# Linear and softmax attention in one kernel: denominators packed by transfers, the keys' mean taken earlier, one state product per tile

## The reference, cut to what matters

```
xn = layernorm(x)                                   # [4, 2048, 512]
# 1: linear attention, 16 heads of 32
q, k = elu(xn @ wq) + 1, elu(xn @ wk) + 1;  v = xn @ wv
for every token: S += k (x) v;  z += k
    num = q . S;   den = q . z + 1e-6;   out1 = num / den
y1 = out1 @ wo
# 2: softmax attention over the whole sequence, 16 heads of 32
q, k, v = xn @ Wq.T + bq, xn @ Wk.T + bk, xn @ Wv.T + bv
q = (q / |q| + query_embedding) * softplus(temperature)
h = softmax(q . k / sqrt(32)) @ v
gates = softmax(h @ Wr.T + br), top 3, times a shared gate of softmax(h @ Ws.T + bs)
y2 = (h * sum(gates)) @ Wp.T + bp
result = x + y1 + y2
```

## Time and profile before

| | us |
|---|---|
| median of 3 | 4643.3 |
| profiled execution | 4645.28 |
| its span | 4643.5 |
| PE busy | 4076.4 (88%) |
| DVE busy | 3418.9 (74%) |
| ACT busy | 2650.1 (57%) |
| mean granted PE clock | 0.955 of full |

### The profile page before, as it was taken

The page is one execution under the profiler, slowest core; times in us unless marked ns, Lnnn a source line. Parts: engine busy times, 40 slices in busy tenths (PEclk is TensorE's granted clock), DMA queues, the critical chain, the costliest instruction groups (busy, mean ns, idle before and its releaser), DMA issues.

```text
span 4643.5 us, 94232 instructions
## 1 busy us (share of the span) xinstructions
PE 4076.4 (88%) x39532; PEld 1690.4 (36%) x39532; DVE 3418.9 (74%) x3549; ACT 2650.1 (57%) x3447; POOL 337.0 (7%) x210
## 2 busy tenths in 40 slices
PE   3489989898989999898999989899998989899768
PEld 1243333333333334333333433333343334333213
DVE  4537888887877878777787877788677767777773
ACT  3126666666656566565666656566665656566550
POOL 0100000000000000000000000000000000000001
PEclk7589999999999999999999999999999999999998
DMA  3421211112222212213221222322122121212115
GB/s 126 134 76 44 58 51 53 57 50 62 61 60 64 82 55 79 63 56 88 64 82 56 79 63 56 88 65 79 47 71 62 51 75 57 76 42 61 33 31 185
DMA packets 368043, 318.15 MB, mean 69 GB/s; under 512 B 157632, under 2 KB 316352, under 8 KB 366912
## 3 DMA queue, kind: packets, MB, share of 16 engines
q1 hardware_dynamic: 367552, 311.32, 22.9%
HBM read 236.25 MB, written 74.97 MB: 67 GB/s over the span
## 4 chain that ended last, share of the span: by engine, by line
PE 54%; DVE 14%; ACT 12%; issue 10%; DMA 9%; SPq 1%; POOL 0%; ACTq 0%; DVEq 0%
PE ps L912 10%; PE ps L926 10%; PE ps L795 10%; ACT prob L669 9%; DVE acc L1393 8%; PE ps L891 6%; DMA rq<-rq_scratch 6%; PE ps L803 5%; PE ps L843 2%; DMA rq_scratch<-rq_c 2%; PE ps L868 2%; PE ps L865 2%; PE ps L823 2%; PE ps L837 1%; PE ps L851 1%
## 5 line engine op out<-in xcount | busy, mean ns | idle before, releaser
L669 ACT ACTIVATE prob<-ps 128x1024 f32<-128x1024 f32 x2048 | 1984.6, 1023 | 939.3 <-PE ps L912 899.1
L1393 DVE TENSOR_TENSOR acc<-acc,prob 128x2048 f32<-128x2048 f32 x896 | 2047.4, 2285 | 76.4 <-ACT prob L669 63.0
L926 PE MATMUL ps<-prob,v 128*32 128x512 f32 x8192 | 1107.2, 613 | 1.1 <-ACT prob L669 1.1
L912 PE MATMUL ps<-q_hi,k_hi 32*128 32x512 f16 x4096 | 426.0, 388 | 306.5 <-ACT prob L669 230.2
L795 PE MATMUL ps<-x_hi,w_hi 128*128 128x512 f16 x1024 | 412.4, 403 | 9.5 <-issue 8.1
L912 PE MATMUL ps<-q_lo,k_hi 32*128 32x512 f16 x4096 | 415.9, 378 | 2.4 <-issue 2.4
L912 PE MATMUL ps<-q_hi,k_lo 32*128 32x512 f16 x4096 | 415.9, 379 | 2.0 <-issue 2.0
L795 PE MATMUL ps<-x_lo,w_hi 128*128 128x512 f16 x1024 | 408.7, 399 | 0.0
L795 PE MATMUL ps<-x_hi,w_lo 128*128 128x512 f16 x1024 | 407.7, 398 | 0.0
L912 PEld LDWEIGHTS ps<-q_hi,k_hi 32*128 32x128 f16 x4096 | 109.4, 91 | 676.3 <-ACT prob L669 461.8
L891 PE MATMUL ps<-wop_hi,fin 128*128 128x512 f16 x1024 | 325.7, 384 | 16.4 <-DVE st L1367 13.0
(11 more groups left out here) (248 smaller groups left out, 4466.5 us busy)
## 6 DMA issues: line engine op xcount, KB each, us to landing
x_hi<-xhi_scratch SPq DMA_DIRECT2D x64, 512.0 KB, 4.1
x_lo<-xlo_scratch SPq DMA_DIRECT2D x64, 512.0 KB, 5.2
x_in<-in_x SPq DMA_DIRECT2D x64, 256.0 KB, 5.4
rq<-rq_scratch SPq DMA_DIRECT2D x64, 256.0 KB
rdl<-rdl_scratch SPq DMA_DIRECT2D x64, 256.0 KB
rden<-rden_scratch SPq DMA_DIRECT2D x64, 256.0 KB
fin<-hhi_scratch SPq DMA_DIRECT2D x128, 128.0 KB, 3.5
fin<-hlo_scratch SPq DMA_DIRECT2D x128, 128.0 KB, 4.6
```

The source lines that it names most:

```text
L669: s_.activation(prob[i % 3][:, 2 * p:2 * p + 2, :], ps[:, 2 * p:2 * p + 2, :], ACT.Exp, bias=-SHIFT, scale=1.0 / CQK).then_inc(exped, 1)
L912: last = t_.matmul(bank[h], kk[rows32(h), cols128(kt)], qq[rows32(h), :], start=(kk is kh and qq is qh), stop=(kk is kl and not wide))
L926: last = t_.matmul(bank[OUT][rows32(h), :], v[m // NB % 2][:, kt, rows32(h)], prob[i % 3][:, h, :], start=(kt == 0), stop=(kt == TT - 1))
L1393: v_.tensor_tensor(acc[:], acc[:], prob[i % 3][:], ALU.add).then_inc(summed, 1)
```

## The change

The names on the left are the kernel's functions.

- `total` and `linear_den` no longer pack. `total` makes one 512-column product for each head against a column block of ones (`ones_v`), `linear_den` a single 512-column product against `blockden`; every channel row of a head then holds that head's denominator.
- ACT copies both from PSUM (`keep_den`, new, slot 1; `keep_dl` now 512 wide), and SP packs them by two transfers (`pack`, new: 4 rows of 512 to DRAM, back as 16 rows of 128). DVE takes the reciprocals of 16 x 128 values, in slots 2 and 5. Then the same spread as before.
- `numerators` uses one full 128 x 128 state product per tile. For that ACT writes the key-value products into `kvm`, whose off-diagonal blocks are cleared once (`keep_kv`, new, slot 13), and `states` adds from `kvm`. ACT copies the numerators out of X1 (`keep_num`, new, slot 3), and DVE divides that copy.
- `mean_k` and `shift_k` of the next round are done in slots 9 and 10 of the last step of the round before; those of the first round ahead of the steps.
- Slots: `divide_o` from 4 to 6, `split_o` from 4 and 5 to 6 and 7, `divide_h` from 5 to 8, `split_h` from 6 and 7 to 9 and 12, `scale_q` from 9 to 11, `split_q` from 9 and 10 to 12 and 13; in slot 14 the mask before the states; the sum over a tile of x (`sum_x`) from 6 to 7. SP's spread of the query norms is ahead of the stores of h and behind the load of the V weights.

```diff
-        den_l, den_h = sb("den_l", [P, BT, HG, BT, ROWS]), sb("den_h", [P, BT, BT, ROWS])
+        blockden, ones_v = sb("blockden", [P, P]), sb("ones_v", [P, HD])
...
+            def pack(dst, scratch_d, src, out_sem, in_sem, i):
+
+                sp.dma_start(scratch_d, src[::HD, :]).then_inc(out_sem, 16)
+                sp.wait_ge(out_sem, (i + 1) * 16)
+                sp.dma_start(dst[:], scratch_d.rearrange("h (t n) -> (h t) n", t=BT)).then_inc(in_sem, 16)
...
                 if p is not None:
-                    sp.wait_ge(rdl_done, p + 1)
-                    spread(rdl, rdl_d, rdl_c[::ROWS, :], rdl_out, rdl_in, p, o1_ready)
+                    sp.wait_ge(dl_kept, p + 1)
+                    pack(rdl_c, rdl_d, rdl, dl_out, dl_in, p)
...
             def keep_dl(p):
                 act.wait_ge(dl_mm, p + 1)
-                act.wait_ge(rdl_done, p)
-                s_.activation(dl[:], X1[:, 0:P], ACT.Identity, bias=eps1[:, 0:1]).then_inc(dl_kept, 1)
+                act.wait_ge(o1_ready, p)
+                s_.activation(rdl[:], X1, ACT.Identity, bias=eps1[:, 0:1]).then_inc(dl_kept, 1)
+
+            def keep_kv(n):
+
+                act.wait_ge(kv_done, n + 1)
+                if n:
+                    act.wait_ge(state_ready, states_after(n - 1))
+                act.wait_ge(kvm_cleared, 1)
+                for h in range(HG):
+                    ins = s_.activation(kvm[rows32(h), :, h, :], X1[rows32(h), :].rearrange("p (t n) -> p t n", t=BT)[:, :, rows32(h)],
+                                        ACT.Copy)
+                ins.then_inc(kv_kept, 1)
+
+            def keep_num(p):
+                act.wait_ge(num_done, p + 1)
+                act.wait_ge(olo_done, p)
+                s_.activation(o1[:], X1, ACT.Copy).then_inc(num_kept, 1)
...
+            def keep_den(m):
+                act.wait_ge(den_done, m + 1)
+                act.wait_ge(hm_done, m)
+                s_.activation(rden[:], X2, ACT.Copy).then_inc(den_kept, 1)
...
             def total(m):
                 pe.wait_ge(summed, (m + 1) * N_ADDS)
-                for j in range(BT):
-                    for h in range(HG):
-                        last = t_.matmul(X2[rows32(h), 0:P], den_h[:, j].rearrange("p t i -> p (t i)"), acc[:, h, cols128(j)],
-                                         start=(j == 0), stop=(j == BT - 1))
+                for h in range(HG):
+                    last = t_.matmul(X2[rows32(h), :], ones_v[:], acc[:, h, :], start=True, stop=True)
                 last.then_inc(den_done, 1)
 
             def linear_den(n):
                 pe.wait_ge(pz_ready, n + 1)
-                for j in range(BT):
-                    last = t_.matmul(X1[:, 0:P], den_l[:, j].rearrange("p h t i -> p (h t i)"), zc[:, cols128(j)], start=(j == 0),
-                                     stop=(j == BT - 1))
-                last.then_inc(dl_mm, 1)
+                t_.matmul(X1, blockden[:], zc[:], start=True, stop=True).then_inc(dl_mm, 1)
...
                     pe.wait_ge(state_ready, i + 1)
+                    t_.matmul(X1[:, cols128(j)], st[:, i % NST, :], phqT[:, cols128(j)], start=True, stop=True)
                     for h in range(HG):
-                        t_.matmul(X1[rows32(h), cols128(j)], st[rows32(h), i % NST, rows32(h)], phqT[rows32(h), cols128(j)],
-                                  start=True, stop=False)
-                    for h in range(HG):
-                        last = t_.matmul(X1[rows32(h), cols128(j)], vl[:, j, rows32(h)], am[:, h, j, :], start=False, stop=True)
+                        last = t_.matmul(X1[rows32(h), cols128(j)], vl[:, j, rows32(h)], am[:, h, j, :], start=False, stop=True,
+                                         skip_group_check=True)
...
-                        if n is not None and n % NB == 0:
-                            mean_k(n // NB)
                     if kt == 2 and n is not None:
                         if mp is not None:
-                            pe.wait_ge(rden_done, mp + 1)
+                            pe.wait_ge(den_kept, mp + 1)
...
                             if p is not None:
-                                pe.wait_ge(o1_ready, p + 1)
+                                pe.wait_ge(num_kept, p + 1)
...
                         project(X2, LQ_, n, (0, 1))
+                        if n % NB == NB - 1 and n < NBLK - 1:
+                            pe.wait_ge(kl_part, n + 1)
+                            mean_k(n // NB + 1)
...
             def invert_dl(p):
-                dve.wait_ge(dl_kept, p + 1)
-                dve.wait_ge(rdl_out, p * 16)
-                v_.reciprocal(rdl_c[:], dl[:]).then_inc(rdl_done, 1)
+                dve.wait_ge(dl_in, (p + 1) * 16)
+                v_.reciprocal(rdl_c[:], rdl_c[:]).then_inc(rdl_done, 1)
...
             def invert_den(m):
-                dve.wait_ge(den_done, m + 1)
-                dve.wait_ge(rden_out, m * 16)
-                v_.reciprocal(rden_c[:], X2[:, 0:P]).then_inc(rden_done, 1)
+                dve.wait_ge(den_in, (m + 1) * 16)
+                v_.reciprocal(rden_c[:], rden_c[:]).then_inc(rden_done, 1)
```

192 lines of the change are left out of this document (105 added, 87 removed).

## The result

The changed kernel takes 4511.4 us, the median of 4 executions (4503.9 to 4512.1), beside 4643.4 us (4640.8 to 4647.2) for the kernel before on the same chip: ratio 0.9711, with a 95% interval of 0.9694 to 0.9728. The forecast was 4520 us. Its profiled execution took 4503.88 us (span 4502.1 us, mean granted clock 0.966), 141.4 us less than that of before. Two executions far above the others of their kernels (6867 us of the kernel before, 4927 us of the one with late norms, at mean granted clocks of 0.65 and 0.82) are left out of the medians.

A forecast was written before the change was run, and what follows sets the result against it. PE, busy 88% of the span, was taken as the bound, with waits in slots 2, 9 and 10 and DVE pacing slots 11 to 13. Terms summed to -123.6 us from 4645.3, forecast 4520 us, range 4472 to 4588.

The forecast's parts named there:

- Keys' mean and X2: Slot 2 of first steps becomes ordinary without mean and reciprocal wait: -64.6 us, 32.9 gained if the clock still falls.
- Query norms: Slots 9 and 10 stop waiting for the spread: -25 us (ends 0, -49); preparing steps -12, far end -34.
- State products: Slot 3: four full products replace four groups of eight, 0.30 us less per full slot, 63 times: -19 us, end 0.
- Linear denominators: One 512-column float32 product at about 0.90 us replaces 1.09 us, 60 times: -11 us.
- `total`: As many columns as before; a change up to 0.5 us lies under slot 1's 0.56 us wait.
- ACT's copies: New copies, about 2.5 us a step, cost +4 us in slot 14; as rival, they show: 4640 us, chance 0.05.
- DVE's order: Earlier `weigh_z` against `split_h` now ahead of `add_o`, for which PE waits before slot 13's products: 0, far end +36 us.
- Packed denominators: Values arriving through DRAM delay slot 3's exponentials by at worst 1.9 us in 12 steps: 0, far end +23 us.
- End: After the last block, a serial ACT copy 0.61 us, store 1.70 us and load about 2 us: +4 us.
- DVE pacing the step: Rival: slots 11 to 13 give back the norms' gain and `split_h` costs 36 us: 4581 us, chance 0.18.
- the low clock: Rival: the branch between rounds still idles PE, so the second low-clock stretch comes back: 4552 us, chance 0.08.
- late denominators: Rival: packed values reach `invert_dl` in slot 2 late, DVE 3.9 us late in 60 steps: 4754 us, chance 0.07.

The follow-up runs named there:

- the last but one experiment: Changed kernel with grouped products and keys' mean back in slot 1, reciprocal of packed linear denominators moved from slot 2 to 3: 4426.6 us, ratio 0.9543.

## Why the prediction was right, and where its terms were not

*What bounds the kernel.* Right: slots 2, 9 and 10, where PE waited, hold 112.6 of the 141.4 us.

*Keys' mean and X2, -64.6.* Measured -64.7 in slot 2 (83.45 us against 148.12), the clock included. But the mean did not have to move: its place in the last steps costs some 9 us of time (10.8 in slots 9 and 13), which the prediction named (DVE's four operations in slot 10) and priced at nothing. The row for it was there: DVE is full in slots 11 to 13, so four operations ahead of them are late work behind them. The prediction also took the mean and the wait for X2 as one cause; either edit alone frees slot 2.

*Query norms, -25 and -12 in the preparing steps.* The mis-sized term, and the one with most of the gain: -84 us when it is made alone. I took half of the idle time of slots 9 and 10 because DVE's full slots follow. All of it went (-47.9 us with everything in place), slots 11 to 13 gave back 2.4 us only (alone they gained 8.7), and the preparing steps gained 21.0 us, between my 12 and the far end of 34. The reasoning that failed is "full slots follow": a full engine that starts earlier also ends earlier. Slot 14 gained 15.9 us for which there was no term. The late norms alone bring 11.3 of it, but with them back in the changed kernel it stays whole, since ACT's copies free X1 there as well: here too either edit does it. What I should have followed is DVE's own wait, 119.1 us in 64 times, through everything that stands behind it in its list.

*State products, -19.* Wrong in sign: +15.9 us in slot 3, and one of the prediction's own signs of being wrong, full products at 0.35 us or more, is there with 0.42 us. The nearest row was read wrongly: L851's 1.10 us for four is four products of 0.22 us and one change of form, not four times 0.275. Beside 32-column products each full one pays 0.20 us for the change. The prediction's end for this term was 0, since "a price above 0.35 us has no row": no row priced a change of form alone, and the far end should have been left open on that side. The Trainium skill, "TensorEngine Tiling", section Key Properties, says that a change of tiling mode drains TensorE; the prediction drew from it a gain of 0. The runs agree with the rule and give it a price: 0.13 us into the 32-column forms, 0.20 us into the full one, four of each a block.

*Linear denominators, -11.* 1.05 us, not 0.90: the division of the earlier trace rows by four left the change of form out again. In slot 15 it is worth 0.03 us a step, about -2 us. *`total`*: nothing, as said.

*ACT's copies, +4.* Measured nothing: slot 14 of the 16 steps without output tiles takes 3.26 us before and after. The copy of the numerators delays the exponentials of slot 4 by 0.19 us, under full PE slots. *DVE's order, 0.* The number is right by luck: PE waits for `add_o` 10.0 us in 11 times, 10.9 in 10 before, but these are two waits of different origin. The late norms alone take the old wait away altogether. Of the new one, 2.2 us stay when the mean goes back to slot 1: that is the most that `split_h` can cost, against the far end of 36, and the rest is the mean's.

*Packed denominators, 0.* Right by the last but one experiment, though DVE does wait for them, 148.0 us in all: the latest reciprocal starts 8.7 us into its step, ahead of the 10.1 us from which the prediction has it cost time. In ten steps it starts behind the exponentials of slot 1, one of the prediction's signs of being wrong, and that had no price either. *End, +4.* 5.9 us, of which little is shown: in the kernel before with grouped products, whose end was not edited, the same stretch is 4.1 us longer. In the chain the copy takes 0.61 us, the store 1.68, the load 1.47. So the load for which I took 2 us between bounds of 1.70 and 4.84 lies below both.

*The sum.* -123.6 against -141.4 us. Misses of opposite sign make the sum look better than it is, and that is luck. The norms (-37 in two terms, -66.5 in slots 9 to 13 and at the start) were some 29 us too small, and slot 14 (-15.9) and the branch between rounds (-12.7) had no term; the products and the linear denominators were 44 us too large in their favour. The rivals: DVE pacing the step is rejected by slots 11 to 13; of the low clock one stretch a round is left, the branch's, and the second is gone, so that rival falls; ACT's copies and late denominators cost nothing.

## What to carry to other kernels

Follow a wait through the whole list of the engine that makes it: its price is what comes late behind it in every later slot, not only PE's idle time next to it. Put matrix products of one form together before making them larger or fewer; a mean duration of a group holds one change of form, and dividing it by the number of products hides that. When an edit frees a buffer by a copy, ask which other edit of the same change frees it too, and leave out the one that costs. A term that comes out at 0 can be two effects that cancel: only a run with one of them tells. And see how much a stretch varies where nothing was edited before a difference in it is explained.

## What the runs showed of the hardware

- By an estimate from groups of 1 and 4 (0.42 and 1.09 us), and of 4 and 16 (0.35 and 1.01 us), a change of form costs PE 0.20 us into full 128 x 128 products and 0.13 us into 32 x 32 ones; into 128 x 32 ones it is the same within 0.01 us (0.36 and 1.01 or 1.05 us). Six changes fewer in each of 64 blocks were worth 55 us with small state products and 58 us with full ones, over 1% of the time.
- By the same estimate a float32 product of 128 x 128 with 128 columns takes 0.22 us, as much as four 32 x 32 ones on the four row groups (4 x 0.055).
- A reload of 8 KB from DRAM, just stored there, took 1.47 us in the chain.
- In the kernel with the norms back, the granted clock between the scores of slots 11 and 12 of the last steps was 0.56 to 0.85 in 12 of 15, behind PE waits that make slots 9 and 10 take 9.7 us with 6.7 us of work; with the norms late, slot 11 is at 1.00 in all 15.
